# Reordering the gates and projections around the last two chunk inversions of a two-layer adaLN kernel

## The reference

```
def step(S, inp):
    qt, kt, vt, bt, gt = inp
    S = S * jnp.exp(gt)[..., None, None]
    kv = jnp.einsum('bhk,bhkv->bhv', kt, S)
    delta = (vt - kv) * bt[..., None]
    S = S + jnp.einsum('bhk,bhv->bhkv', kt, delta)
    ot = jnp.einsum('bhk,bhkv->bhv', qt, S)
    return (S, ot)
...
g = (hidden_states @ Wg).reshape(b, l, NH, DV)
var = jnp.mean(o * o, axis=-1, keepdims=True)
o = o * jax.lax.rsqrt(var + 1e-05) * g_norm_weight
o = o * g * jax.nn.sigmoid(g)
return o.reshape(b, l, VD) @ Wo
```

## Time and profile before

| | |
|---|---|
| median of 3 runs | 2726.82 us (2725.18 to 2732.91) |
| profiled execution, its own time | 2734.56 us |
| its span | 2732.8 us |
| mean granted TensorE clock | 0.976 of full speed |
| PE busy | 2433.6 us (89%) |
| DVE busy | 1794.9 us (66%) |
| ACT busy | 1455.4 us (53%) |
| Pool busy | 825.4 us (30%) |

### The profile page before, as it was taken

One profiled execution on the slowest core, in us unless ns is written; L12 is line 12 of the kernel. 1 busy time (PEld: TensorE's weight loads), 2 busy tenths in 40 slices (PEclk: granted clock), 3 DMA queues, 4 the chain that ended last, 5 costly groups with the idle time before them and its releaser, 6 DMA issues.

```text
span 2732.8 us, 65917 instructions
## 1 busy us (share of the span) xinstructions
PE 2433.6 (89%) x24299; PEld 1680.0 (61%) x24299; DVE 1794.9 (66%) x4697; ACT 1455.4 (53%) x3129; POOL 825.4 (30%) x581
## 2 busy tenths in 40 slices
PE   3899988899898998989989899899988999889998
PEld 2456765477554775547745577456764567655676
DVE  3467864777737776478655776567864678636776
ACT  0466534755448554385544754457444665446643
POOL 3036210552105520065202542025320363104621
PEclk7999999999999999999999999999999999999999
DMA  8201132011310114001220113201122011220113
GB/s 260 105 1 22 17 99 79 4 20 17 106 71 7 23 21 139 28 13 19 72 108 5 18 17 101 80 1 19 19 98 80 1 20 18 97 80 3 21 16 102
DMA packets 226985, 138.31 MB, mean 51 GB/s; under 512 B 173567, under 2 KB 209799, under 8 KB 219431
## 3 DMA queue, kind: packets, MB, share of 16 engines
q1 hardware_dynamic: 208870, 125.48, 16.2%
q10 hardware_dynamic: 17780, 8.39, 1.1%
HBM read 95.10 MB, written 38.71 MB: 49 GB/s over the span
## 4 chain that ended last, share of the span: by engine, by line
PE 50%; DVE 18%; ACT 15%; issue 8%; DMA 6%; SPq 2%; POOL 2%; ACTq 0%; DVEq 0%; POOLq 0%
PE bank L914 7%; PE bank L699 4%; PE bank L509 4%; PE bank L690 3%; DVE small L1367 3%; PE bank L1013 3%; PE bank L622 3%; ACT arena L1638 3%; ACT arena L1637 2%; PE bank L952 2%; DVE blk_tx L1369 2%; ACT vq L1645 2%; PE bank L547 2%; DVE mx L1171 2%; PE bank L602 2%
## 5 line engine op out<-in xcount | busy, mean ns | idle before, releaser
L1925 POOL TENSOR_TENSOR arena<-upto,gk 128x1536 f32<-128x1536 f32 x32 | 88.1, 2754 | 682.8 <-DVE beta L1308 682.8
L1315 DVE SCALAR_TENSOR_TENSOR arena<-bank,conv,arena 128x510 f32<-128x510 f32 x320 | 237.1, 747 | 45.1 <-ACT arena L1638 26.1
L509 PE MATMUL bank<-mask_k,ident_bf 128*128 128x512 bf16 x976 | 250.8, 391 | 0.0
L1171 DVE TENSOR_REDUCE mx<-bank 128x2 f32<-128x768 f32 (+3 forms) x187 | 201.5, 1123 | 47.2 <-PE bank L548 46.1
L1917 POOL TENSOR_TENSOR arena<-arena 128x511 f32<-128x511 f32 x160 | 201.8, 1272 | 56.8 <-DVE arena L1315 56.8
L1601 ACT ACTIVATE arena<-bank 128x384 f32<-128x384 f32 (+1 forms) x384 | 168.5, 544 | 49.3 <-PE bank L607 49.2
L760 PE MATMUL bank<-h_pad,arena 128*128 128x512 f32 x320 | 165.6, 615 | 28.7 <-DVE arena L1315 21.8
L547 PE MATMUL bank<-vq 128*128 128x512 bf16 (+3 forms) x544 | 123.2, 313 | 55.3 <-issue 32.9
L1367 DVE TENSOR_TENSOR small<-blk_tx,blk 96x1 f32<-96x1 f32 (+14 forms) x480 | 142.8, 297 | 16.5
L1622 ACT ACTIVATE arena<-bank,b1e 128x512 f32<-128x512 f32 x128 | 87.8, 686 | 116.8 <-PE bank L690 111.6
L1276 DVE SCALAR_TENSOR_TENSOR arena<-bank,comb,arena 128x128 f32<-128x128 f32 x256 | 72.0, 344 | 114.9 <-PE bank L699 113.7
(11 more groups left out here) (300 smaller groups left out, 5912.1 us busy)
## 6 DMA issues: line engine op xcount, KB each, us to landing
vq<-q_rows SPq DMA_DIRECT2D x18, 1024.0 KB, 7.6
vq<-k_rows SPq DMA_DIRECT2D x18, 1024.0 KB, 10.9
arena<-w_bounce SPq DMA_DIRECT2D x16, 1024.0 KB, 6.0
q_rows<-qkp SPq DMA_DIRECT2D x81, 128.0 KB, 2.4
k_rows<-qkp SPq DMA_DIRECT2D x81, 128.0 KB, 2.4
arena<-wv_rows SPq DMA_DIRECT2D x8, 768.0 KB, 10.1
ogt<-wv_rows SPq DMA_DIRECT2D x8, 768.0 KB, 11.7
t_bounce<-blk_tx SPq DMA_DIRECT2D x32, 192.0 KB, 2.1
```

The lines of the kernel that those rows point to most:

```text
L509: mm(PS[bank][:, :], ident_bf[:, :], mask_k[:, :, :].rearrange("p h w -> p (h w)"), start=True, stop=True)
L1171: V.reduce_max(dst, unit_scores(u), AX.X).then_inc(s_max, 1)
L1315: ins = V.scalar_tensor_tensor(a[:, k:T], ps[:, 0:T - k], conv[:, n, 3 - k:4 - k], a[:, k:T], ALU.mult, ALU.add)
```

## The change

- TensorE: `levels(3)` comes directly after `turn_out(1)`. The three groups of chunk 2's gates and the projection of chunk 1 stood between them, and are now inside `levels(3)`: four heads of the projection ahead of step 1, eight ahead of step 3, and one gate group ahead of each of steps 4, 6 and 7. The eight extra matmuls of `levels(3)` are gone.
- Two of chunk 1's three gate groups stay ahead of `levels(2)`, and the third is between its steps 0 and 1. The extra matmuls of `levels(2)` are 4, 3, 3 and 2 ahead of steps 3, 4, 6 and 7 (they were 4, 2 and 2 ahead of 3, 4 and 6).
- DVE: `project(0)` goes from before `attend(3)` to behind `levels(2)`, `rms(1)` from behind `attend(3)` to before it, and `project(1)` from before `levels(3)` to behind `enter_stats(1)`.
- ACT: `rms(1)` comes before `gate(1)`. `gate(2)` goes from before `levels(3)` to behind `rms(2)`, directly before `gate(3)`, and the two share one pair of table loads.
- Pool: `gate_keys(3)` is left out, and with it ACT's copy of chunk 3's keys.
- Banks and waits follow: `unknowns(2)` waits for `project(0)`, `gate(3)` for the end of `levels(3)` and for `project(1)`, and `levels(3)` no longer waits for `project(1)`.

```
@@ banks
         def qk2_banks(c):
-            return few_banks if c < 2 else PS[3:6]
+            return few_banks if c < 2 else PS[3:6] if c == 2 else [PS[4], PS[5], PS[6]]
...
-            return [PS[6], PS[6], PS[1], PS[0]][c]
+            return [PS[3], PS[6], PS[1], PS[0]][c]
...
-            return [[PS[7], PS[6], PS[2]], [PS[7], PS[2], PS[6]], [PS[2], PS[7], PS[6]], [PS[3], PS[6], PS[7]]][c]
+            return [[PS[7], PS[6], PS[2]], [PS[7], PS[2], PS[6]], [PS[2], PS[7], PS[3]], [PS[4], PS[5], PS[6]]][c]
@@ pe_stages
-                      ("outputs", 1), ("turn_out", 0), ("gram", 3), ("project", 0), ("attend", 3), ("gate_first", 1), ("gate", 1)]
+                      ("outputs", 1), ("turn_out", 0), ("gram", 3), ("project", 0), ("attend", 3), ("gate_first", 1)]
         pe_stages += [("levels", 2), ("key_part", 2), ("query_part", 2), ("unknowns", 2),
-                      ("outputs", 2), ("turn_out", 1), ("gate_first", 2), ("project", 1), ("gate", 2)]
-        pe_stages += [("levels", 3), ("enter_norm", 1), ("gate_first", 3), ("gate", 3), ("enter_qkv", 1),
+                      ("outputs", 2), ("turn_out", 1)]
+        pe_stages += [("levels", 3), ("enter_norm", 1), ("gate", 3), ("enter_qkv", 1),
                       ("key_part", 3), ("query_part", 3), ("unknowns", 3), ("outputs", 3),
@@ act_stages
-        act_stages += [("gate", 1), ("rms", 1), ("levels", 2), ("query_part", 2), ("unknowns", 2), ("project", 1)]
-        act_stages += [("gate", 2), ("levels", 3), ("rms", 2), ("enter_norm", 1), ("enter_h", 1), ("gate", 3),
+        act_stages += [("rms", 1), ("gate", 1), ("levels", 2), ("query_part", 2), ("unknowns", 2), ("project", 1)]
+        act_stages += [("levels", 3), ("rms", 2), ("gate", 2), ("gate", 3),
@@ dve_stages
-                       ("outputs", 1), ("gram", 3), ("project", 0), ("attend", 3), ("rms", 1)]
-        dve_stages += [("levels", 2), ("subst", 3), ("differences", 2), ("scale", 1), ("outputs", 2), ("project", 1)]
-        dve_stages += [("levels", 3), ("enter_stats", 1), ("rms", 2), ("enter_norm", 1), ("enter_h", 1), ("scale", 2), ("enter_qkv", 1),
+                       ("outputs", 1), ("gram", 3), ("rms", 1), ("attend", 3)]
+        dve_stages += [("levels", 2), ("project", 0), ("subst", 3), ("differences", 2), ("scale", 1), ("outputs", 2)]
+        dve_stages += [("levels", 3), ("enter_stats", 1), ("project", 1), ("rms", 2), ("enter_norm", 1), ("enter_h", 1), ("scale", 2), ("enter_qkv", 1),
@@ pool_stages
-        pool_stages += [("decay_state", 1), ("scale_decays", 3), ("rms", 1), ("gate_keys", 3), ("scale_v", 3)]
+        pool_stages += [("decay_state", 1), ("scale_decays", 3), ("rms", 1), ("scale_v", 3)]
@@ levels(c) on TensorE
                         pe.wait_ge(o_ready, at(b, o_ready, NG * c))
-                        pe.wait_ge(wo_done, at(b, wo_done, c - 1))
                     for s in range(8):
-                        keep_warm(3, {3: 4, 4: 2, 6: 2}.get(s, 0))
+                        if c < 2:
+                            keep_warm(3, {3: 4, 4: 2, 6: 2}.get(s, 0))
+                        elif c == 2:
+                            if s == 1:
+                                gate_group(1, 2)
+                            elif s == 3:
+                                pe.wait_ge(gate_ready, at(b, gate_ready, NG + 1))
+                            keep_warm(7, {3: 4, 4: 3, 6: 3, 7: 2}.get(s, 0))
+                        elif c == 3 and s in (1, 3):
+                            project(1, range(0, 4) if s == 1 else range(4, HD))
+                        elif c == 3 and s in (4, 6, 7):
+                            gate_group(2, (4, 6, 7).index(s))
@@ gate_first(c), then gate_proj(c), on TensorE
                     gate_group(c, 0)
+                    if c == 1:
+                        pe.wait_ge(gd_ready, at(b, gd_ready, NG * NT))
+                        gate_group(c, 1)
...
+                        pe.wait_ge(lv_sb, at(b, lv_sb, L_SB * NT))
+                        gate_group(c, 0)
                         gate_group(c, 1)
+                        pe.wait_ge(wo_done, at(b, wo_done, 2))
                         gate_group(c, 2)
@@ unknowns(c) on TensorE
+                    if c == 2:
+                        pe.wait_ge(wo_done, at(b, wo_done, 1))
@@ gate_silu(c) on ACT
-                    nc.scalar.preload_act_table_set("silu_and_others")
+                    if c + 1 < NT:
+                        nc.scalar.preload_act_table_set("silu_and_others")
...
-                    nc.scalar.preload_act_table_set(EXP_LN)
+                    if c != 2:
+                        nc.scalar.preload_act_table_set(EXP_LN)
```

More of the change, by code:

```diff
@@ L27 @@
     "qkv_t": 20, "vt_ps": 8, "v_tok": 8, "vd_ps": 4, "vd_ready": 4, "gm_ready": 4, "small_ps": 1, "kt_ps": 8, "qt_ps": 8, "dec_ready": 1,
-    "k_sq": 8, "q_sq": 8, "k_ss": 4, "q_ss": 4, "k_norm": 4, "q_norm": 4, "beta_ready": 4, "v_scaled": 4, "kd_ready": 4, "lower_ps": 16, "l_ps": 12,
+    "k_sq": 8, "q_sq": 8, "k_ss": 4, "q_ss": 4, "k_norm": 4, "q_norm": 4, "beta_ready": 4, "v_scaled": 4, "kd_ready": 3, "lower_ps": 16, "l_ps": 12,
     "dt_ready": 12, "g_ps": 12, "gd_ready": 12, "qk2_ps": 12, "pt_ready": 12,
@@ L930, in gate_proj @@
                         gate_group(c, 2)
-                    elif c + 1 < NT:
-                        if c == 1:
-                            pe.wait_ge(gd_ready, at(b, gd_ready, NG * (c + 3)))
+                    else:
+                        pe.wait_ge(lv_sb, at(b, lv_sb, L_SB * NT))
+                        gate_group(c, 0)
                         gate_group(c, 1)
[L935 to L939, removed]
+                        pe.wait_ge(wo_done, at(b, wo_done, 2))
                         gate_group(c, 2)
@@ L1027, in turn_out, with project @@
                         last.then_inc(og_ps, 1)
-                def project(c):
+                def project(c, lot=range(HD)):
                     ps = wo_bank(c)
-                    pe.wait_ge(ogt_ready, at(b, ogt_ready, NG * (c + 1)))
-                    for h in range(HD):
+                    if lot.start == 0:
+                        pe.wait_ge(ogt_ready, at(b, ogt_ready, NG * (c + 1)))
+                    for h in lot:
                         last = mm(ps[:, 0:D], ogt[:, h, :], wo[:, h, :], start=(h == 0), stop=(h == HD - 1))
-                    last.then_inc(wo_ps, 1)
+                    if lot.stop == HD:
+                        last.then_inc(wo_ps, 1)
                 walk = {"conv": convolve, "tile": tile, "direct": direct, "tokens": to_tokens, "keys": keys, "queries": queries, "mask": mask, "gram": gram, "attend": attend,
@@ L1701, in keys @@
                 def keys(c):
-                    if c:
+                    if c and c + 1 < NT:
                         act.wait_ge(kd_ready, at(b, kd_ready, c))
@@ L1706, in keys @@
                         ps = k_banks(c)[i]
-                        A.copy(ktok[:, 512 * i:512 * i + n], ps[:, 0:n])
+                        if c + 1 < NT:
+                            A.copy(ktok[:, 512 * i:512 * i + n], ps[:, 0:n])
                         A.activation(squares(c)[0][:, 512 * i:512 * i + n], ps[:, 0:n], ACT.Square).then_inc(k_sq, 1)
```

## The result

The changed kernel took 2699.2 us (median of four runs, 2691.6 to 2706.4), the kernel before beside it 2729.9 us (2725.2 to 2736.7): a ratio of 0.987 (95% interval 0.983 to 0.992), so it is faster by 30.6 us. In two later sets of runs it had ratios of 0.989 (0.986 to 0.993) and 0.991 (0.988 to 0.994). The forecast was 2698.0.

The account below looks back on a forecast made before the run. The prediction took TensorE's path (PE busy 89%) as the bound, with ACT leading from the end of levels(3). Terms 13.1 + 2 + 20 = 35 us off 2734.56 gave 2699.6, forecast as 2698 us, range 2681 to 2716.

Parts of the forecast that it names:

- levels(3): From turn_out(1) to Pool's first part: levels(3) starts 6.44 us earlier and takes 16.0; 1.63 us a pass, 13.1 in all.
- levels(2): Chunk 1's inversion: step 1 follows step 0 at once, more extra matmuls; 0.25 us less a pass, 2 us in all.
- ACT's row: On ACT from the last copy of levels(3) to Pool's first part: three more SiLUs (1.57 us), so about 7.1 us.
- Rival two: ACT's tail behind levels(3): six SiLUs in a row cost 3.1 us a pass, not 1.6; total 2710; chance 0.11.
- Two table loads fewer: On ACT before levels(3), where it had idled: the saved loads are not on the path, counted as nothing.
- The clock: In both stretches, levels(3)'s and levels(2)'s: up to 26.4 us lost at the lower clock may return; 20 us taken.
- the sum of 35: Whole kernel: 13.1 + 2 + 20 = 35 us off the profiled execution's 2734.56.

Follow-up runs that it names:

- the short tail: The changed kernel, but each of chunk 2's three SiLUs covers one head of four, the other heads' gates left out: 2698.0 us, ratio 0.985.
- the group ahead: The changed kernel, but chunk 1's third gate group stands ahead of levels(2), not at its step 1: 2705.6 us beside 2704.8 for the change.

## Why the prediction was right

*`levels(3)`.* Its step 0 starts directly behind `turn_out(1)`; 16.2 us to `enter_norm` against 16.0; the wait ahead of `enter_qkv` 0.58 against 0.8; the last copy 1006.62 - 989.73 = 16.89 behind `turn_out(1)` against 16.65; ACT's row from there to Pool's part 1013.59 - 1006.62 = 6.97 against 7.15; the stretch 23.86 against 23.8. Over the undisturbed passes of before (25.43 by the prediction's mean) that is 12.6 us against 13.1. Rival two, gaps between the SiLUs, falls: six ran back to back, three in 1.57 us and three in 1.60. But it was right on what matters there, as the short tail shows: what is saved on ACT is gained in full.

*Two table loads fewer* were priced at nothing, because they weren't on the path. The load that stayed on it was worth having: moving that one and `rms(2)` into the inversion gave 0.9 us a pass.

*`levels(2)`: the step that failed.* The prediction took a margin of 0.3 us between DVE's scaling and PE, and a gain of 0.25 us a pass. It set DVE's end at 963.95 with the small operations of `rms(1)` at their price with Pool idle. But moved ahead of `attend(3)` they run beside Pool's `scale_v(3)` and `decay_state(2)`, and last until each ends: 1.5 us more for two instructions. I had weighed just this for `project(0)`, where the earlier trace rows show 2.10 against 0.29, and it came out at 0.29 there (L1473, 969.53); for the four instructions next to it I hadn't asked which engine runs beside them. The stretch became 0.4 us longer, not 0.25 shorter: 3.4 us over eight passes, and 4.1 with the first two, against -2. With Pool's work later, the shorter stretch of 25.4 that the order allows is there. The Trainium skill (SBUF — State Buffer, section "SBUF: two separate sides") says that GpSimd and a DVE instruction with two SBUF inputs, or in a 2-port mode, lock one pair of ports against each other for a whole instruction. The trace agrees: both slow instructions end 0.03 us behind one of Pool's, and beside the same Pool instruction TENSOR_REDUCE (1.74, one SBUF input) takes what it took in the earlier trace rows. L1358 (1.89 for three, one input from PSUM), with Pool at work too, takes what L1363, of the same form, takes with Pool idle. L1439 has one SBUF input, so by the page it would have to be in a 2-port mode, which no run here shows.

*The clock.* I took 20 of the 26.4 us that the two stretches had lost. All of it came back, in these stretches: 13.1 behind `turn_out(1)`, 13.3 around `levels(2)`. That it was the filler's doing, and not chance or the order alone, is shown from three sides: the old order with more filler holds 1.00 in sixteen of sixteen windows, `levels(2)` without its four new extras falls in four of eight passes, and the same gates bunched let `levels(3)` fall in eight of eight. What I didn't foresee is that other stages gave 7.4 us back in the first profile. So 12.6 + 26.4 - 4.1 = 34.9 in the stretches, 28.4 in the whole. That the sum of 35 was met is luck: its errors offset each other (the clock +6.4, `levels(2)` -6.1), and the forecast of 2698.0 is so near the median of 2699.2 for that reason. The mechanism behind `turn_out(1)` was right as predicted.

The Trainium skill (TensorE: Matmul & The Clock Gate, section "HAM oscillation — how this bites in real kernels") ties such falls to long waits for DMA. Ahead of the first pass the trace agrees. There PE waited 14.22 us for a load of weights, and the mean clock over the wait was 0.60 (kernel before, PE's row and the window of the wait):

```profile
45.34 4.96 PE L564 MATMUL bank<-ident,arena 128*128 128x128 f32 x22 [14.22 <-DMA arena<-in_L_ffn_W_dram]
```

```profile
31.08:45.30 14.22, 0.05 (x1) 0.00 (x0) 0.69 (x1) 0.00 (x0) 11.70 (x10) 0.60 0.92 315
```

In the two stretches it isn't the cause: with the gates bunched, PE never waited longer than 0.71 us in the last steps, for ACT, and the clock fell all the same.

*What stays open.* The single falls with Pool's work later and with the group ahead (one pass of eight each, one profile each) can't be put down to their edits. Nor is it settled which property of the spread filler holds the clock, only that its place matters: the bunched gates also opened waits of 0.4 to 0.7 us, and the two weren't tried apart. And why the clock fell more often between scores and gates in the changed kernel's first profile, where it lost 7.4 us, was not tried.

## What to carry to other kernels

Independent matmuls are worth more spread one by one over the waits of a chain of small dependent steps than in one block ahead of it or at its start: they cover the waits, take the place of idle filler, and keep the clock up; bunched, the same matmuls lost most of the gain (2727.7 us against 2704.2, where the kernel before has 2734.9). When an instruction is moved, look at what runs on the neighbouring engine at its new place, small ones too: two DVE operations of 12 columns cost 1.5 us beside Pool. And where runs of one kernel differ by 10 us, measure an edit from event to event in every pass; 0.5 us a pass is plain there and invisible in the medians.

## What the runs showed of the hardware

- DVE instructions that take 0.17 us took 0.46 and 1.39 beside Pool, up to the end of Pool's instruction; the reduction and the reads from PSUM next to them kept their time.
- The mean granted clock was 0.81 to 0.87 in every pass with `levels(3)`'s gates bunched. In one of them PE had been busy 13.94 of the 14.51 us up to the fall. A busy PE is no sign of a held clock.
- ACT's table load took 1.28 us wherever it stood, and copies (L1769) ran with the SiLU table in place, without another load.
